# Linear attention: negative parts on ScalarE, the output's two additions apart, and a new stagger of the chunk steps

## What is computed

```
h = h + _L0_attn_ref(_layernorm(h), ...)

q = einsum('bnc,oc->bno', x, Wq)         # 8 heads of 8
k, v likewise from Wkv
q = elu(q) + 1.0
k = elu(k) + 1.0
D_inv = 1.0 / maximum(einsum('bhnd,bhd->bhn', q, k.sum(axis=2)), 1e-06)
context = einsum('bhnd,bhne->bhde', k, v)
attn = einsum('bhnd,bhde->bhne', q, context) * D_inv[..., None]
out = einsum('bnc,oc->bno', attn, Wproj) + bproj
```

## Time and profile before

| | us |
|---|---|
| median of three runs | 698.66 |
| the profiled execution, its own time | 692.95 |
| span of the profile | 691.0 |
| linear attention, first TensorE instruction to last VectorE instruction | 54.30 to 108.31 |
| in that stretch: TensorE and VectorE busy, of the whole run | 85%, 70% |
| mean granted TensorE clock over the run | 0.925 |

### The profile page before, as it was taken

How to read it: one execution, slowest core, us unless ns; L and a number is a source line. 1 busy time by engine, 2 the same in 40 slices (tenths; PEclk the granted TensorE clock), 3 DMA queues, 4 the chain that set the end, 5 groups by cost and what they waited for, 6 DMA issues and landing times. The chain is left out here.

```text
span 691.0 us, 13147 instructions
## 1 busy us (share of the span) xinstructions
PE 585.3 (85%) x4778; PEld 385.8 (56%) x4778; DVE 486.1 (70%) x1352; ACT 310.5 (45%) x659; POOL 252.3 (37%) x220
## 2 busy tenths in 40 slices
PE   6995777978876979899899999998697979988886
PEld 5774666756643523222587877887132233987453
DVE  0455667867466796888647888587757898954695
ACT  1431433745556534355234655323232438943174
POOL 6756971131002210110175686553301138800150
PEclk9998898999985599999999999999897999999998
DMA  6877622020000200000100000004000010000002
GB/s 187 237 249 200 186 67 81 3 66 0 1 1 0 83 0 1 0 1 0 42 8 8 15 9 8 15 1 135 17 1 0 1 42 1 2 3 2 0 1 62
DMA packets 18944, 30.06 MB, mean 44 GB/s; under 512 B 6466, under 2 KB 15810, under 8 KB 18242
## 3 DMA queue, kind: packets, MB, share of 16 engines
q1 hardware_dynamic: 16322, 19.81, 10.1%
q0 software_dynamic: 2560, 9.44, 4.7%
HBM read 27.26 MB, written 1.05 MB: 41 GB/s over the span
## 5 line engine op out<-in xcount | busy, mean ns | idle before, releaser
L177 POOL TENSOR_TENSOR norm_rstd<-norm_var,minus_half 128x16 f32<-128x16 f32 x16 | 47.1, 2943 | 174.5 <-DVE norm_var L171 174.5
L1413 ACT ACTIVATE m_g<-PS,w_slot 128x512 f32<-128x512 f32 x96 | 60.8, 685 | 85.2 <-PE PS L1464 85.2
L1358 DVE TENSOR_TENSOR m_gw<-m_g,PS 128x512 f32<-128x512 f32 x96 | 60.9, 675 | 16.7 <-PE PS L1472 7.9
L1464 PE MATMUL PS<-m_xT,w_slot 64*128 64x512 f32 x192 | 61.9, 653 | 0.7 <-ACT m_g L1413 0.5
L1488 PE MATMUL PS<-m_gw,w_slot 128*64 128x512 f32 x192 | 56.1, 654 | 1.2 <-DVE m_gw L1358 1.2
L106 PE MATMUL PS<-w_base 128*128 128x128 f32 x350 | 51.5, 296 | 5.6 <-DMA w_base<-in_w_base 4.2
L106 PEld LDWEIGHTS PS<-w_base 128*128 128x128 f32 x350 | 43.0, 152 | 12.6 <-issue 5.7
L1472 PE MATMUL PS<-m_gT,m_sel 48*128 48x512 bf16 x96 | 24.8, 409 | 18.6 <-DVE m_gw L1358 15.0
L147 DVE BATCH_NORM_STATS2 norm_halves<-H 128x6 f32<-128x64 f32 x256 | 34.6, 211 | 3.4 <-PEq L2906 3.1
L1472 PEld LDWEIGHTS PS<-m_gT,m_sel 48*128 48x128 bf16 x96 | 5.9, 93 | 53.1 <-DVE m_gw L1358 41.3
L262 POOL DMA_INDIRECT tok_windows<-in_emb,tok_ids x32 | 30.5, 953 | 11.2 <-issue 9.4
(11 more groups left out here) (341 smaller groups left out, 1489.8 us busy)
## 6 DMA issues: line engine op xcount, KB each, us to landing
rff_routed<-in_routed SPq DMA_DIRECT2D x64, 129.0 KB, 2.5
w_slot<-in_w_rat SPq DMA_DIRECT2D x1, 1525.0 KB, 10.9
w_slot<-in_w_win SPq DMA_DIRECT2D x1, 1378.5 KB, 6.0
w_slot<-in_w_m SPq DMA_DIRECT2D x1, 1329.0 KB, 5.7
w_slot<-in_w_early SPq DMA_DIRECT2D x1, 1100.0 KB, 5.0
rat_inv<-in_rat_taps SPq DMA_DIRECT2D x1, 1024.0 KB, 7.6
rat_hf<-in_rat_taps SPq DMA_DIRECT2D x1, 1024.0 KB, 8.0
out<-H SPq DMA_DIRECT2D x8, 128.0 KB, 2.2
```

Of the source, the lines that this page charges most:

```text
L177: nc.gpsimd.tensor_tensor(N.rstd[:], N.var[:], C.minus_half[:], ALU.pow).then_inc(S["norm_rstd"], 1)
L1358: nc.vector.tensor_tensor(gw[:, i % 2, half, :], g[:, i % 2, half, :], gate_bank[half], ALU.mult)\
L1413: nc.scalar.activation(g[:, i % 2, half, :], hid_bank[(n - 1) % 3], ACT.Gelu, bias=b1[:, s:s + 1])\
L1464: nc.tensor.matmul(hid_bank[n % 3], w1[lane(half), s, :], pair_of(xT, pair)[lane(half)], start=True, stop=True).then_inc(S["hid_ps"], 1)
```

## The change

Three things are done, in this one stage.

1. `negative_parts` moves from VectorE to ScalarE. It now writes relu(-x) of the scores, and `exponentials` takes exp(-1 times that), which is the same number. So ScalarE makes two passes of 128x512 for a chunk, and VectorE loses one.
2. `add_output` is split: `add_bias` keeps tick 75, and the addition onto H comes 7 ticks later, behind the next chunk's `elu` and `divide`.
3. The offsets are new on all three engines. The second half's `norm_stats` goes from tick 27 to tick 2, ahead of the first `elu`; `norm_centre` comes at tick 29; the next stage's `norm_halves` follow the later addition.

```diff
-            def negative_parts(c):
-                w = c % W
-                v.wait_ge(S["qk_ps"], c + 1)
-                nc.vector.tensor_scalar(neg[:, w], PS[w][:, 0, :].rearrange("p (a n) -> p a n", a=2),
-                                        0.0, None, ALU.min).then_inc(S["neg"], 1)
...
-            def add_output(c):
+            def add_bias(c):
                 w = c % W
                 v.wait_ge(S["proj_ps"], c + 1)
                 y = groups(PS[w][:, 1, 0:CW])
                 nc.vector.tensor_tensor(y, y, bcast(C["lin_b"], 1, G4), ALU.add).then_inc(S["proj"], 1)
+
+            def add_output(c):
                 v.wait_ge(S["proj"], c + 1)
...
             def then(n):
-                if n == 27:
+                if n == 2:
                     norm_stats(nc, v, S, hx(1), N, 1)
+                if n == 29:
                     norm_centre(nc, v, S, hx(1), N, xc)
...
-            ladder([(34, mask_context), (14, negative_parts), (75, add_output), (22, elu), (54, divide)], 28, then)
+            ladder([(34, mask_context), (75, add_bias), (22, elu), (52, divide), (82, add_output)], 28, then)
...
+            def negative_parts(c):
+                w = c % W
+                act.wait_ge(S["qk_ps"], c + 1)
+                nc.scalar.activation(neg[:, w], PS[w][:, 0, :].rearrange("p (a n) -> p a n", a=2), ACT.Relu,
+                                     scale=-1.0).then_inc(S["neg"], 1)
+
...
-                nc.scalar.activation(neg[:, w], neg[:, w], ACT.Exp).then_inc(S["expneg"], 1)
+                nc.scalar.activation(neg[:, w], neg[:, w], ACT.Exp, scale=-1.0).then_inc(S["expneg"], 1)
...
-            ladder([(3, copy_xT), (62, copy_aT), (17, copy_v), (19, exponentials), (78, normalise)], 28)
+            ladder([(3, copy_xT), (14, negative_parts), (72, copy_aT), (19, exponentials), (23, copy_v), (82, normalise)], 28)
...
-            ladder([(0, turn_x), (30, context), (60, turn_attended), (8, queries_keys), (15, values), (73, project),
+            ladder([(0, turn_x), (30, context), (4, queries_keys), (62, turn_attended), (9, values), (73, project),
                     (46, attention)], 28)
```

More of the change, by code:

```diff
@@ L437, in elu @@
                 v.wait_ge(S["expneg"], c + 1)
+                v.wait_ge(S["qk_ps"], c + 1)
                 nc.vector.scalar_tensor_tensor(qk[:, w].rearrange("p a n -> p (a n)"), PS[w][:, 0, :], 0.0,
@@ L462, in add_output @@
                 nc.vector.tensor_tensor(y, y, bcast(C["lin_b"], 1, G4), ALU.add).then_inc(S["proj"], 1)
+            def add_output(c):
                 v.wait_ge(S["proj"], c + 1)
                 x = groups(H[:, c * CW:(c + 1) * CW])
-                nc.vector.tensor_tensor(x, x, y, ALU.add).then_inc(S["h_new"], 1)
+                nc.vector.tensor_tensor(x, x, groups(PS[c % W][:, 1, 0:CW]), ALU.add).then_inc(S["h_new"], 1)
             def then(n):
-                if n == 27:
+                if n == 2:
                     norm_stats(nc, v, S, hx(1), N, 1)
+                if n == 29:
                     norm_centre(nc, v, S, hx(1), N, xc)
-                if 75 <= n < 75 + W * 28 and n % 28 == 19:
-                    w = (n - 75) // 28
+                if 83 <= n < 83 + W * 28 and n % 28 == 27:
+                    w = (n - 83) // 28
                     v.wait_ge(S["h_new"], w + 1)
```

## The result

The changed kernel takes 694.44 us (median of 20 runs) against 698.11 us for the kernel before in the same runs: 3.7 us less, a ratio of 0.9943 with a 95% interval of 0.9921 to 0.9965. One of the 20 executions took 729.74 us at a mean granted clock of 0.794, a slow state that the ratio leaves out, and without it the median is 693.36 us, 4.8 us less. The forecast was 691.4 in a range of 688.0 to 695.5. The direction and the range held, and the gain is half to two thirds of the forecast 7.3 us.

The account below looks back on a forecast made before the run. The prediction took a ring of short waits through three engines to bound the stage, with GpSimd's end as the new floor: 7.8 us gained less 0.5 gives 7.3, so 698.66 - 7.3 = 691.4 us, range 688.0 to 695.5.

Parts of the forecast that it names:

- The ring: Chain of waits per chunk through TensorE, ScalarE and VectorE in the linear attention stage: 4.55 us instead of 5.37.
- The start: Stage start: statistics moved ahead of the first elu, first mask_context 3.3 us earlier, second elu at 62.3.
- The statistics are hidden: Stage start: VectorE's 3.03 us of statistics and sums fit its idle time before ScalarE's exponential ends at 58.45.
- the forecast's cover of 2.3 us: Stage end: VectorE's gain beyond GpSimd's end, lost from the saving but kept as cover for slow clock.
- The end: Stage end: arithmetic done at 98.2, 10.1 us earlier, but GpSimd ends at 100.49, so the stage gains 7.8 us.
- It becomes the last to arrive: Barrier at the stage's end: GpSimd, set by an unchanged DMA, ends at 100.49, after VectorE at 98.2.
- the forecast's own sign of being wrong: Stage end: VectorE's last instruction later than 101 would show the forecast wrong.
- three rings at low clock: TensorE at 1.2 GHz lengthens each ring by 1.8 us; three give 694.5. Whole arithmetic-last clock rival: chance 0.16.
- the forecast's own ends of 689.0 to 692.8: Next stage's start: 1.9 us given back or lost through TensorE's low clock, around the forecast total.
- The clock in mid-stage: Rivals with TensorE at 1.2 GHz in the ring: arithmetic last, 692.7 to 698.1, chance 0.16; slower, 701.2 or 701.7, 0.05.
- table load: Rival: ScalarE reloads tables between relu and exp, 20.5 us in the ring, about 709 us; chance 0.01.
- The 0.5 us for a slow start of the next stage: Cost taken for TensorE's longer idle ahead of the next stage, which starts at low clock.

Follow-up runs that it names:

- the three moves: Changed kernel with GpSimd's second-half root before its first addition, eighth addition in the next stage, next stage's root before the sixth: 686.64 us, ratio 0.9836 to before.
- without the last addition: Changed kernel without GpSimd's last 128x2048 addition in the stage, except for 8 columns, its DMA wait kept: 691.86 us.
- root first: Changed kernel with GpSimd's root for the second half ahead of its first addition: 696.81 us.
- both moves: Changed kernel with GpSimd's second-half root ahead of its first addition and its eighth addition moved into the next stage: 691.69 us, ratio 0.9902 to before.

## Why the prediction came out as it did

**The ring: right.** 4.42 against 4.55, by the steps that the forecast listed; the pass was 0.60 instead of 0.69. The rule of "ScalarE: Activation LUTs" in the Trainium skill, that relu belongs on VectorE, was judged by the pass alone, and there the trace stays against it (597 ns on ScalarE, 0.69 us on VectorE). Its advice came out right in the ring, but not by the speed that the page gives for it: back on VectorE the period fell by 0.27 us, because the pass no longer stood ahead of `copy_aT`.

**The start: a wrong step.** "The statistics are hidden" failed. The step took 3.03 us from a row in which GpSimd was idle and put it beside GpSimd's first addition. GpSimd in the kernel before, the first addition and the wait that followed:

```profile
54.71 4.16 POOL L652 TENSOR_TENSOR rff_routed<-rff_routed,rff_shared 128x2048 f32<-128x2048 f32 x1 [0.40 <-DVE rff_shared L486]
...
62.70 3.03 POOL L177 TENSOR_TENSOR norm_rstd<-norm_var,minus_half 128x16 f32<-128x16 f32 x1 [3.65 <-DVE norm_var L171]
```

The forecast put the statistics and sums at 54.57 to 57.6, beside that addition, which ran from 54.71 to 58.87. The 3.03 us became 5.15, and the first `elu` came 5.35 us after the first transpose instead of 58.5 - 54.3 = 4.2. The second `elu` was at 10.47 instead of 8.0, since TensorE's clock was at 1.2 GHz for 10.3 us as well: from the first `elu` to the second it took 5.12 us, and 3.73 with the three moves, where the low spell had ended by then. That this spell was so long because of the hold is likely and not shown: in three of the four kernels with the hold it lasted 10 us, in the others at the start at most 7, but the fourth, without the last addition, had two short ones. By the end of the ring VectorE was 1.9 us behind the forecast (its last `elu` at 37.19 instead of 89.6 - 54.3 = 35.3). Against a floor at GpSimd's end alone, the forecast's cover of 2.3 us would have absorbed that.

**The end: this is the step that cost the gain.** "It becomes the last to arrive" had VectorE finished at 98.2, that is 43.9 after the first transpose, and GpSimd at 100.49, 46.2. GpSimd did end near there, 47.1. But VectorE was not done: it was held in its centring until GpSimd's addition had ended, and 2.75 us of its work (102.40 to 105.15) came behind GpSimd's last instruction. So VectorE was the last to arrive, by the forecast's own sign of being wrong: its last instruction came 49.87 us after the first transpose, which is 104.2 on the forecast's time axis, later than 101. The forecast put the next stage's first VectorE instruction 47.3 us after the first transpose, and it came at 50.95. The 3.7 us between them are 2.75 of VectorE's work behind GpSimd's end and 0.9 of a later GpSimd (its DMA wait ended 0.77 later, and its small addition took 0.41 instead of 0.23). That is the difference between the stage's forecast gain of 7.8 and the measured 4.1, and about as large as what is missing in the medians. A start as forecast would not have avoided a hold. The forecast's eighth `elu` at 89.6 puts the centrings at 94.7 to 96.1, just ahead of the addition at 96.13, and the scalings, which have two SBUF inputs too, beside it; this is an estimate from rows, and no run shows it.

**The range: held by luck.** Its high end of 695.5 stood for three rings at low clock, and in mid-stage, from 66.9 to 97.6, none came. The measured total lies in that upper part, above the forecast's own ends of 689.0 to 692.8, and the hold that made the stage longer stands nowhere in the forecast.

**The rivals.** None of them named this wait. The clock in mid-stage was at the high level, as the forecast argued. No table load came. GpSimd ended the stage, but through VectorE's hold and not through the barrier. The 0.5 us for a slow start of the next stage can't be told apart from the spread.

## What to carry to other kernels

A duration read in a row holds for the company that the instruction had there. Before moving an instruction, look up what runs on the other engines at its new place, and for VectorE beside GpSimd count the inputs in SBUF: two inputs beside GpSimd's long addition meant a wait for that addition's end in every trace here. When one engine becomes the last at a barrier, check that the work of the others can finish beside it.

Which part of a change gains is told by taking parts back one at a time: here the order of steps gained, and the move between engines, which looks like the main thing, cost a little in most periods, with the new order in place.

## What was not expected of the hardware

- The hold lasts to the end of GpSimd's instruction whatever the size of the held one: sums of 16 columns took 2.16 to 3.03 us instead of 0.18, and one centring of 256 columns was held until GpSimd's whole 4.16 us were over.
- Not every long GpSimd instruction holds: beside the root of 128x16, which takes 2.92 us from 60.80 on, the centring at 61.24 took its usual 1.42. The small addition of 128x16 did prolong a hold once: with the root first, the held sum got through at 86.86, when that addition (86.56 to 86.82) had ended and not when the long one had (86.63).
- The same kernel's total runs from 687.88 to 697.56 us over the executions compared, at mean granted clocks of 0.930 and 0.914. A held VectorE instruction can cost more than its own length through TensorE's clock: where the sums for the next stage were held, 3.0 us instead of 0.18, the clock fell to 1.2 GHz, and the two periods took 4.5 us (root first: 6.92 and 6.40) and 4.8 us (both moves) more than two of 4.43. At the stage's end, where no ring follows, the hold cost its own length.
